# Where the first sums of a mixture of experts stand in GpSimd's program, and four experts' sections written out

## The reference

```python
xn = layernorm(x)
s = recurrent_layer(xn)                          # gated recurrence of 8 states, projections
scores = softmax(xn @ wg.T)                      # 32 experts, the 4 best of the 4 best groups of each token
dest = expert * 1280 + position_in_expert        # each expert holds at most 1280 rows
for e in range(32):                              # every expert on its own rows
    out[e] = (silu(xe[e] @ w1[e]) * (xe[e] @ w3[e])) @ w2[e] * weight
y = zeros.at[token].add(out)                     # each token sums its (up to) 4 experts
z = silu(xn @ sw1) * (xn @ sw3) @ sw2            # an expert that all tokens share
result = x + s * silu(y + z)
```

## Time and profile before

| | us |
|---|---|
| median of three executions | 1065.22 |
| lowest, highest | 1063.51, 1071.57 |
| the profiled execution's own time | 1065.27 |
| its span, first to last instruction | 1063.5 |
| PE busy in the span | 996.5 (94%) |
| POOL busy in the span | 727.3 (68%) |
| DVE busy in the span | 775.2 (73%) |

### The profile page before, as it was taken

The page is one execution under the profiler, slowest core; times in us unless marked ns, Lnnn a source line. Parts: engine busy times, 40 slices in busy tenths (PEclk is TensorE's granted clock), DMA queues, the critical chain, the costliest instruction groups (busy, mean ns, idle before and its releaser), DMA issues.

```text
span 1063.5 us, 29638 instructions
## 1 busy us (share of the span) xinstructions
PE 996.5 (94%) x8031; PEld 949.1 (89%) x8031; DVE 775.2 (73%) x2475; ACT 548.7 (52%) x1039; POOL 727.3 (68%) x573
## 2 busy tenths in 40 slices
PE   8789999998989977999999998999999999999975
PEld 6788889898889976999999998999999999999932
DVE  6878888878788854767777675676777777767664
ACT  4767787787654432444444444444444444444444
POOL 4077777777777777778888885766666666666440
PEclk8989999999999998999999999999999999999987
DMA  9763434443476878989899988878798989878879
GB/s 254 221 215 137 142 142 142 148 143 137 142 246 214 244 208 172 212 164 176 162 195 205 182 165 173 199 154 199 157 198 197 209 185 197 165 142 176 222 204 349
DMA packets 179382, 199.31 MB, mean 187 GB/s; under 512 B 20769, under 2 KB 171090, under 8 KB 179282
## 3 DMA queue, kind: packets, MB, share of 16 engines
q1 hardware_dynamic: 124992, 126.70, 40.0%
q0 software_dynamic: 53696, 71.50, 35.4%
q10 hardware_dynamic: 594, 0.01, 0.0%
HBM read 96.89 MB, written 104.90 MB: 190 GB/s over the span
## 4 chain that ended last, share of the span: by engine, by line
PE 53%; DMA 3%; issue 2%; POOL 2%; DVE 1%; ACT 1%; DVEq 0%; POOLq 0%; SPq 0%; ACTq 0%
PE h L1088 11%; PE h L1090 11%; PE h L1089 10%; PE yb L1108 5%; PE yb L1106 5%; PE yb L1107 5%; PE xt L1072 5%; DMA y_sum<-y_more,y_idx 2%; POOL y_sum L899 2%; POOL slot_rows L921 0%; DVE s_all L2119 0%; DMA x_all<-slot_rows 0%; DMA w_hl<-y_sum 0%; DMA slot_rows<-x_all 0%; DVE s_all L2123 0%
## 5 line engine op out<-in xcount | busy, mean ns | idle before, releaser
L1088 PE MATMUL h<-xh,w_hl 128*128 (+1 forms) x1392 | 410.1, 295 | 4.7 <-DVE xl L1714 3.1
L1090 PE MATMUL h<-xl,w_hl 128*128 (+1 forms) x1392 | 393.3, 283 | 0.0
L1089 PE MATMUL h<-xh,w_hl 128*128 (+1 forms) x1392 | 392.0, 282 | 0.0
L1438 ACT ACTIVATE acth<-act 128x512 fp32r<-128x512 f32 x174 | 109.9, 632 | 334.9 <-PE yb L1108 289.7
L1088 PEld LDWEIGHTS h<-xh,w_hl 128*128 128x128 f32 x1392 | 263.5, 189 | 7.3 <-issue 6.6
L1089 PEld LDWEIGHTS h<-xh,w_hl 128*128 128x128 f32 x1392 | 263.7, 189 | 0.0
L1090 PEld LDWEIGHTS h<-xl,w_hl 128*128 128x128 f32 x1392 | 263.4, 189 | 0.0
L1724 DVE TENSOR_TENSOR actl<-act,acth 128x512 fp32r<-128x512 f32 x174 | 120.7, 694 | 173.1 <-ACT acth L1438 172.7
L1106 PE MATMUL yb<-w_hl,acth 128*128 128x256 f32 x692 | 197.6, 286 | 2.7 <-DVE actl L1724 0.5
L1108 PE MATMUL yb<-w_hl,actl 128*128 128x256 f32 x692 | 195.6, 283 | 0.0
L1107 PE MATMUL yb<-w_hl,acth 128*128 128x256 f32 x692 | 195.2, 282 | 0.0
(11 more groups left out here) (253 smaller groups left out, 1601.8 us busy)
## 6 DMA issues: line engine op xcount, KB each, us to landing
rows<-slot_rows SPq DMA_DIRECT2D x122, 289.0 KB, 3.9
raw<-L_ffn_w SPq DMA_DIRECT2D x99, 256.0 KB, 2.9
slot_rows<-rows SPq DMA_DIRECT2D x32, 289.0 KB
x_all<-L_attn_x SPq DMA_DIRECT2D x16, 512.0 KB, 6.8
x_all<-L_attn_x SPq DMA_DIRECT2D x32, 256.0 KB, 4.4
out<-s_all SPq DMA_DIRECT2D x32, 256.0 KB, 4.1
y_sum<-yw SPq DMA_DIRECT2D x31, 256.0 KB
x_all<-slot_rows SPq DMA_DIRECT2D x20, 289.0 KB, 4.2
```

Of the source, the lines that this page charges most:

```text
L1088: mm(out, high, xh[:, k, cols], start=(k == 0), stop=False)
L1089: mm(out, low, xh[:, k, cols], start=False, stop=False)
L1090: ins = mm(out, high, xl[:, k, cols], start=False, stop=(k == KD - 1))
L1438: av(acth[:, :], act[:, :], ACT.Copy).then_inc(acth_ready, 2)
```

## The change

It has four parts.

1. On POOL the sums of expert 0's two pairs move behind the last scatter.
2. POOL's sums come in another order: the fourth (and fifth) pair of expert 4 is summed right behind its third, ahead of expert 5's first pair, where before it came behind all of expert 5. PE, ACT and SP keep their order, and so does DVE, so this pair is computed after expert 5's. The waits around experts 4, 5 and 6 follow the new neighbours.
3. DVE's wait for a fifth pair's buffer names other sums: experts 8 to 10 wait only for the early pair that was in the buffer (before, for `fifth_added` as well), expert 7 for nothing, and experts 11 to 20 for the fifth pairs of experts four or more before, not two or more before.
4. The loop of experts 12 to 19 is written out on POOL and on DVE. Two operations of `count_apart` on DVE go.

```diff
@@ gpsimd: scatters
                 for t in range(GT):
-                    if g == GROUPS - 1 and t == GT - 1:
-                        pool.wait_ge(z_stored, 16 * (A_PAIRS - 1))
-                        pool.wait_ge(last_z_stored, 16)
-                        add_early(0)
-                        add_early(1)
                     for k in range(K):
                         pool.indirect_dma_start(
...
+            pool.wait_ge(z_stored, 16 * (A_PAIRS - 1))
+            pool.wait_ge(last_z_stored, 16)
+            add_early(0)
+            add_early(1)
@@ gpsimd: section
-                        add_pair(home, first_added)
+                        add_pair(home if first_home is None else first_home, first_added)
+                        if first_home is not None:
+                            pool.reg_add(count.pairs, count.pairs, 1)
+                            pool.reg_add(count.pairs, count.pairs, count.behind[FIRST - 2])
+                            pool.wait_ge(apart_added[FIRST - 1], pool.snap(apart_needed))
...
@@ gpsimd: early sums
+            def add_fourth(e, pairs_before):
+
+                pool.wait_ge(apart_added[e], early_adds(e))
+                pool.reg_add(count.pairs, count.behind[FIRST - 1], EARLY_PAIRS + 1)
+                with pool.If(count.flag_behind(e) > 0):
+                    add_pair(SET_A + PAIRS, fifth_added, PAIRS)
+                add_pair(SET_A, apart_added[e])
+                pool.reg_mov(count.pairs, pairs_before)
+
...
-                    pool.wait_ge(apart_added[e - 1], early_adds(e - 1))
+                    if e == FIRST - 1:
+                        pool.reg_add(apart_needed, shared, early_adds(e - 1))
+                        pool.wait_ge(apart_added[e - 1], pool.snap(apart_needed))
+                        pool.wait_ge(fifth_added, fifth_adds(count.fifths_now()))
+                    else:
+                        pool.wait_ge(apart_added[e - 1], early_adds(e - 1))
                     pool.wait_ge(third_added[(e - 1) % 2], third)
                 add_early(q)
                 if e > 1 and j == 0:
                     pool.wait_ge(third_added[(e - 1) % 2], third_adds(e - 1))
-            behind_fifth = count.flag_behind(FIRST - 1)
-            with pool.If(behind_fifth > 0):
+                    if e == FIRST - 1:
+                        pool.wait_ge(apart_added[e - 1], early_adds(e - 1) + 32)
+                if (e, j) == (FIRST - 2, 2):
+                    add_fourth(e, q + 1)
+            pool.wait_ge(apart_added[FIRST - 1], early_adds(FIRST - 1))
+            with pool.If(count.flag_behind(FIRST - 1) > 0):
                 add_pair(BEHIND_FIFTH, apart_added[FIRST - 1])
-            add_pair(BEHIND_LAST, apart_added[FIRST - 1])
-            pool.wait_ge(third_added[(FIRST - 1) % 2], third_adds(FIRST - 1))
-            hold(apart_added[FIRST - 1], 32 * behind_fifth + early_adds(FIRST - 1) + 32)
-            with pool.If(count.flag_behind(FIRST - 2) > 0):
-                add_pair(SET_A + PAIRS, fifth_added, PAIRS)
-                pool.reg_mov(fifth_behind, 1)
-            for e in range(FIRST, CYCLE_START + CYCLE):
-                section(e, y_set(e), y_set(e - 1) if e > FIRST else None, set_uses(e - 1) + 1)
-            with pool.Fori(0, (CYCLE_END - CYCLE_START) // CYCLE - 1) as i:
-                for n in range(CYCLE):
-                    section(i * CYCLE + CYCLE_START + CYCLE + n, CYCLE_SETS[n], CYCLE_SETS[n - 1], i + 2)
-            for e in range(CYCLE_END, CYCLE_END + 2):
+            pool.reg_mul(apart_needed, count.behind[FIRST - 1], 32)
+            pool.reg_add(apart_needed, apart_needed, early_adds(FIRST - 1))
+            section(FIRST, y_set(FIRST), None, 0, first_home=BEHIND_LAST)
+            for e in range(FIRST + 1, CYCLE_END + 2):
                 section(e, y_set(e), y_set(e - 1), set_uses(e - 1) + 1)
@@ vector: section
-                ve.reg_mov(ahead_fifths, last_fifths)
-                ve.reg_mov(last_fifths, count.fifths_now())
+                for n in range(CYCLE - 1, 0, -1):
+                    ve.reg_mov(fifths_before[n], fifths_before[n - 1])
+                ve.reg_mov(fifths_before[0], count.fifths_now())
+                early_set = isinstance(e, int) and e < CYCLE_START + CYCLE - 1
+                behind = 1 if not isinstance(e, int) or e > CYCLE_END else 0 if e == FIRST else CYCLE - 1
...
-                        free, landed = fifth_added, fifth_adds(ve.snap(ahead_fifths))
...
+                        free, landed = fifth_added, fifth_adds(ve.snap(fifths_before[behind]))
@@ vector: experts
-            for e in range(FIRST, CYCLE_START + CYCLE):
+            for e in range(FIRST, CYCLE_END + 2):
                 section(e, (e + 1) % 2, y_set(e), lambda slot, e=e: free_wait(e, slot), FIRST - 2 if e == FIRST else None)
-            with ve.Fori(0, (CYCLE_END - CYCLE_START) // CYCLE - 1) as i:
-                for n, home in enumerate(CYCLE_SETS):
...
```

More of the change, by code:

```diff
@@ L932, in shared_adds, with section @@
                 return pool.value_load(may_share[0:1, bass.ds(e, 1)], min_val=0, max_val=32)
-            def section(e, home, ahead, ahead_uses):
+            def section(e, home, ahead, ahead_uses, first_home=None):
                 shared = shared_adds(e)
@@ L941, in body @@
                     elif slot == 0:
-                        add_pair(home, first_added)
+                        add_pair(home if first_home is None else first_home, first_added)
[3 more added lines that the diff above has]
+                            pool.wait_ge(apart_added[FIRST - 1], pool.snap(apart_needed))
+                            pool.reg_mov(third_needed, shared)
+                            pool.reg_add(third_needed, third_needed, third_adds(FIRST - 1) - 32)
+                            pool.wait_ge(third_added[(FIRST - 1) % 2], pool.snap(third_needed))
                         pool.reg_mov(first_needed, shared)
@@ L963, in body @@
                             pool.wait_ge(first_added, first_adds(e))
+                            if first_home is not None:
+                                pool.wait_ge(third_added[(FIRST - 1) % 2], third_adds(FIRST - 1))
                             if ahead is not None:
@@ L972, in _ @@
             count.load_flags()
+            apart_needed = pool.alloc_register("pool_apart_needed")
+            def add_fourth(e, pairs_before):
[5 more added lines that the diff above has]
+                pool.reg_mov(count.pairs, pairs_before)
             for q in range(EARLY_COUNTS[0], EARLY_PAIRS):
@@ L1895, in count_apart @@
                                                   ALU.is_ge, ALU.mult))
-                own, behind = slice(FIRST, FIRST + 1), slice(FIRST - 2, FIRST - 1)
-                count_link(v.scalar_tensor_tensor(apart[:, own], before_border[:, own], float(PAIR), late[:, behind],
-                                                  ALU.is_ge, ALU.mult))
                 v.tensor_scalar(may_share, apart, -1.0, 32.0, ALU.mult, ALU.add).then_inc(counts_ready, 1)
@@ L2016, in pair @@
                 count.next(slot)
-            ahead_fifths, last_fifths = ve.alloc_register("dve_ahead_fifths"), ve.alloc_register("dve_last_fifths")
-            ve.reg_mov(ahead_fifths, 0)
-            ve.reg_mov(last_fifths, 0)
+            fifths_before = [ve.alloc_register(f"dve_fifths_before{n}") for n in range(CYCLE)]
+            for register in fifths_before:
+                ve.reg_mov(register, 0)
             def free_wait(e, slot):
@@ L2027, in free_wait @@
                     of, j = EARLY_LIST[1 if e == FIRST else 2 + y_set(e) - SET_B + slot]
-                    return ((first_added, first_adds(FIRST)) if of == FIRST - 1 else
-                            (third_added[of % 2], third_adds(of)) if j == 2 else (apart_added[of], early_adds(of)))
+                    return (third_added[of % 2], third_adds(of)) if j == 2 else (apart_added[of], early_adds(of))
                 if slot == 0:
-                    return first_added, first_adds(e - (5 if e == CYCLE_START + CYCLE - 1 else 4 if e == CYCLE_END else 2))
+                    return first_added, first_adds(e - (CYCLE + 1 if e == CYCLE_START + CYCLE - 1 else CYCLE if e <= CYCLE_END else 2))
                 return added[y_set(e) // SET][slot], slot_adds(slot, set_uses(e))
@@ L2038, in section @@
             def section(e, w_slot, home, waits, y_before=None):
-                ve.reg_mov(ahead_fifths, last_fifths)
-                ve.reg_mov(last_fifths, count.fifths_now())
+                for n in range(CYCLE - 1, 0, -1):
[3 more added lines that the diff above has]
+                behind = 1 if not isinstance(e, int) or e > CYCLE_END else 0 if e == FIRST else CYCLE - 1
                 def body(slot):
                     fifths = count.fifths_now()
-                    if slot == PAIRS:
-                        if isinstance(e, int) and e < CYCLE_START + CYCLE - 1 and e != FIRST + 1:
-                            ve.wait_ge(*waits(slot))
```

(7 more changed lines are left out.)

## The result

| | before | after |
|---|---|---|
| median, us | 1065.85 (6 executions) | 1054.98 (6 executions, 1051.34 to 1057.8) |
| profiled execution's own time, us | 1065.27 | 1052.09 |
| its span, us | 1063.5 | 1050.3 |

The ratio is 0.9891, with a 95% interval of 0.9862 to 0.992. The forecast was 1053.1, in a range of 1050.5 to 1059.0. Executions of one kernel differ by several us, mostly with the mean granted clock of the execution: it is 0.983 in the changed kernel's fastest (1051.34) and 0.974 in its slowest (1057.8).

A forecast was written before the change was run, and what follows sets the result against it. PE was taken as the bound, working 94% of the span, with losses at a row load and at expert 15 to 16. 1063.5 - 7.55 - 4.66 = 1051.3 us, plus 1.77 outside the span, gave 1053.1; range 1050.5 to 1059.0.

The forecast's parts named there:

- lower end: At the row load: the smallest gain forecast from moving expert 0's sums, 6.1 us against 7.55.
- the slow clock "cancels": On PE after the row-load stop: half speed costs 1.5 us before and after the change alike.
- landing and load keep their length: At the row load: the last scatter still lands in 2.54 us and the rows in 3.74 us.
- rival (a): At the row load: load queues behind zeros or SP comes late, gain 4 us or less, 1056.5 to 1058; chance 0.12.
- (b): At expert 15 to 16: DVE's stop moves instead of going, only the moved sums gain, 1057.7; chance 0.09.
- (d): Experts 16 to 19: straight code stops DVE in each section, costing 18.6 us, 1071.7; chance 0.03.
- POOL's backlog: POOL's queued sums: they run further behind DVE but delay nobody, and the backlog ends about 660 to 680 us.
- the start of the sums: On POOL behind the moved sums: its next sum starts 2 to 5 us after its 400.12.
- Rival (c): POOL's backlog reaches DVE through a wait with under 17 us of room (closest found 46), 1055 to 1060; chance 0.07.
- The sum: Whole kernel: gains of 7.55 at the row load and 4.66 at expert 15 to 16, giving 1053.1 us.
- its line of 1%: Whole kernel: a measurement tells about 1% from no change, 10.65 us, so faster means below 1054.6 us.
- the wait with under 4 us of room: DVE at expert 8's fifth buffer: the old wait would stop DVE some 4 to 8 us once it runs earlier.

The follow-up runs named there:

- number 2: Kernel before with expert 0's sums moved and the new wait for a fifth buffer, order of sums and loops as before: 1059.28 us, ratio 0.9966.
- number 1: Kernel before with only expert 0's sums moved behind the last scatter: 1068.4 us, ratio 1.0052.
- number 10: Changed kernel without the new order of sums, expert 4's fourth pair summed behind all of expert 5 as before: 1057.14 us, ratio 0.991.
- number 11: Changed kernel run once more, unaltered: 1054.79 us, ratio 0.9897.
- number 3: Kernel before with the loop of experts 12 to 19 written out on DVE alone: 1061.32 us, ratio 0.9972.
- number 4: Kernel before with the loop of experts 12 to 19 written out on POOL alone: 1065.05 us, ratio 1.0012.
- Numbers 3 to 5: number 3, number 4, and the changed kernel with DVE's late loop of two sections made one of four: 1061.94 us, ratio 0.9978.
- numbers 6 to 8: Changed kernel with 64 constant products in PE's row-load gap, 1053.17 us; with flags read in the gap, 1049.59; with early flags and 48 products, 1051.59.
- number 9: Changed kernel with flags read in the gap, 48 constant products there, and DVE's sections written out to expert 31: 1046.84 us, ratio 0.9852.

## Why the prediction came out

**Part 1** was forecast at 7.55 us, with a lower end of 6.1. The path was the one named: scatter, landing, load, PE. The last scatter moved as forecast: it starts 2.1 us ahead of PE's stop in four of the five kernels with the move and 0.9 in number 2, 1.9 in the mean, and 6.7, 5.2 and 5.2 us behind it in the three without the move, 5.7 in the mean, so 7.6 us earlier. But the pairs round the row load take only 6.66 us less, as the mean of those five (7.19, 6.81, 6.09, 6.63, 6.56), and the three kernels without the move are themselves 0, 1.72 and 2.30 below, 1.34 in the mean. That leaves 6.66 - 1.34 = 5.3 us, under my lower end. The step that failed first is that the slow clock "cancels": PE works at half clock for 4.7 to 6.1 us after the gap in the kernels with the move, for 2.8, 4.6 and 3.1 without it, which at half speed is 1.1 us more on average. The second is that landing and load keep their length. The row load takes 3.40, 4.48, 3.12, 4.12 and 4.30 us with the move (the changed kernel, numbers 1, 2, 10 and 11; mean 3.9) and 3.74, 2.80 and 2.95 without (before, numbers 3 and 4; mean 3.2), and the scatter lands in 3.27, 2.80, 3.87, 3.02 and 2.89 us with it (mean 3.2) and in 2.54, 2.50 and 2.53 without: together 1.4 us. 7.6 - 1.1 - 1.4 = 5.1 accounts for the 5.3 measured. SP was not late: it was at its wait for the scatters before the last one landed in all of them, though by less than 0.1 us in number 1. So rival (a) is there in small, at 1.4 us and not at its own price; that it is the neighbouring transfers that lengthen landing and load fits these rows, but no run took them away.

**Part 2** was forecast at nothing, and is nothing (number 10).

**Part 3** was forecast to gain nothing and to keep part 1 whole, at 4 to 8 us of DVE's time. Number 1 shows it: DVE stops 4.71 us, PE loses 6.1, and part 1 alone is slower than before by half a per cent.

**Part 4**: 4.66 forecast, 4.65 measured, 4.68 on DVE alone; with POOL alone the stop is still there. The 1.5 us of slow clock in the 4.66 belongs to the execution that was profiled: number 4 has the stop without it. Numbers 3 to 5 show that it is DVE's jump over four sections. The Trainium skill (Runtime: NRT & Kernel Launch, Instruction fetch mechanics) has the matching rule, that a taken branch out of the code held waits for a fetch; the traces show the idle time (3.69 and 5.87 us at the long turns, 0.4 to 0.9 at the short ones), and that it was a fetch is argued, not shown. Rivals (b) and (d) fall: in number 3 PE has no wait in straight code.

**POOL's backlog** reached nobody, as forecast, but it was sized wrong. I gave it an end near 660 to 680, without a sum; by POOL's timeline it lasts to 697. The term at fault is the start of the sums: 402.85 lies in the 402 to 405 forecast, but this execution reached the first mark 2.96 us earlier. Counted from that mark the sums start 12.9 us behind it and not 9 to 12; counted from the last scatter, 16.1 us and not 11 to 14. Whether that makes the whole difference isn't shown. POOL idles 7.62 us there. Its wait for the landing and its reading of the flags, which starts at 399.6, follow each other now; before, the flags were read while the scatters still ran, as the last section shows. Rival (c) has 17 us as its worst case, and 46 us of room made that harmless.

**The sum** was 12.2 us. The runs make it 5.3 + 4.65 - 0.3 = 9.6 us, the last term being the late short turns, whose pairs take 0.5 to 0.7 us longer in the changed kernel and in numbers 6 to 8, 10 and 11, though their code is the same, less the 0.3 to 0.4 us that the pairs ahead of them gain. The medians give 10.87 us and, on the chip of number 11, 1063.25 - 1054.79 = 8.5. So the direction and both places were right, part 4 to the tenth, and part 1 was 2.2 us too large, since it took one execution's stop for the stop and its clock and transfers as unchanged. That the median came within 1.9 us of the forecast all the same is in part luck of the executions: against the 8.5 us the sum would look worse. The prediction also gave 0.62 to a gain clear of its line of 1%; the measured gain is 1.1%, with an interval of 0.8 to 1.4%, so that call was not borne out.

## What to carry to other kernels

When a change makes one engine earlier, go through every wait whose other side becomes later, and give each its room in us: here the wait with under 4 us of room would have eaten the gain, and before neither DVE nor PE ever stopped at it. A stop can cost more than its idle time, since PE mostly comes back at half clock (not at the turn in number 4); work that has to be done anyway (here, reading flags) belongs into the gap. A loop whose body is several sections long can stop its engine at each turn, and a chain of waits with "issue" in front of the first instruction of a body is where to look.

## What the runs showed of the hardware

The time at half clock does not follow the length of the gap: 2.8 us of PE's work after 13.2 us without any, 3.1 after 11.0, 4.6 after 10.8, 5.9 after 4.8, 3.0 after 2.6, none after 3.05 (the turn in number 4), and none after 1.0. What decides between these stays open.

A turn over four sections cost DVE 3.7 to 4.4 us at one place and 5.9 at another. And the short turns of the loop of two sections, idle DVE 0.6 to 0.9 us in the changed kernel and 0.4 to 0.5 before, with the same code in the loop. I don't know why. Not all of it is the turn: with the sections written out (number 9) DVE still idles 0.3 us at the same places.

POOL's program ran ahead of its DMA instructions. In the chain of the kernel before, from 396.5 to 399, lines 493 and 494 of `load_flags`, which stands behind all scatters, lie ahead of the last scatter's start at 398.56:

```profile
397.68 0.30 POOLq L493
...
398.24 0.10 POOLq L494
```

With the sums moved, the wait for their landing stands between the two, and POOL idles 7.6 us that no row of before had shown as a cost.
